# A two-layer transformer on one core: the last tile's rotation and the output weights' split move from the first attention into its projection

## The chip, the core and the metric

The kernel runs on one core of a Trainium2 chip. The metric is the device time of one execution in microseconds (us). The engines are named as in the profile: PE does matrix multiplies, DVE, ACT and POOL do elementwise work, SP starts DMA transfers. They run side by side and wait for each other by semaphores.

## What is computed

Two pre-norm layers, each with attention and a feed-forward block, on x of 2 x 512 tokens x 512, all in float32:

```python
x = L0_attn_x
x = x + _L0_attn_ref(_layernorm(x), Wq, Wk, Wv, Wo)
x = x + _L0_ffn_ref(_layernorm(x), ...)      # gated, low-rank corrections
x = x + _L1_attn_ref(_layernorm(x), ...)     # 32 heads of 128
x = x + _L1_ffn_ref(_layernorm(x), ...)      # gated
```

The change lies in the first of these lines. There, with 32 query heads and 8 key-value heads of 16:

```python
q, k, v = x @ Wq, x @ Wk, x @ Wv             # split into heads
q, k = _apply_rope(q, cos, sin), _apply_rope(k, cos, sin)
scores = einsum('bhqd,bhkd->bhqk', q, k_h) / sqrt(16)     # causal mask
ctx = einsum('bhqk,bhkd->bhqd', softmax(scores), v_h)
return ctx @ Wo
```

## The kernel before, in words

The 1024 tokens are 8 tiles of 128 rows (NT = 8; QT = 4 tiles to a batch element). To keep float32 accuracy, each operand of a multiply is held as a rounded high part and the remainder as a low part: ACT copies the high part (`..._hi`), POOL or DVE subtracts it from the original for the low part (`..._lo`), and PE makes three passes.

`project0` (L912 to L1137) is the first stage. DVE takes the moments of the rows (L97 to L102), ACT takes the root, DVE finishes the inverse (L110 to L114) and writes the normalised row of 512 (`ln.rows`, L140). PE transposes it into `p_turned` (L186), ACT and DVE split it into `h0_hi` and `h0_lo` (L170, L153), and PE multiplies with the query columns (`p_qbank`, 512 wide) and with the key and value columns (`p_kvbank`, 256 wide). Moments are taken for pairs of tiles (PARTS). In program order, DVE takes those of tiles 0 to 3 ahead of the first rotation, those of tiles 4 and 5 behind the first, those of tiles 6 and 7 behind the second. Then, tile by tile, DVE rotates the query columns (`rotate_part`, L892, L896, L897: a cosine product in `rot_a`, a sine product in `rot_b`), then the key columns; POOL adds both products over all 640 columns in one instruction (L1134); ACT writes the high parts of query (L1023) and key (L1025) twice; DVE writes the query's low part (`query_low`, L902) and POOL the key's (`key_low`, L909). `rot_a` and `rot_b` have two buffers. `fill` writes the constant columns, on DVE that of `q2` (512 wide, L1066) among them.

The last tile (LATE = 7) is only copied off PSUM by ACT (L1047, L1048). Its rotation is done within `attend0`, on DVE in unit 1 (`late_rotate`), on POOL (L1853, L909), on ACT (L1722, L1724), and its query low on DVE in unit 2.

`attend0` (L1140 to L1868) begins when every engine has left `project0`: each stage is a block, and between two stands a barrier. It works through 8 units (a batch element and two of its key-value heads), in an order that is written out by hand and identical on each engine. A unit has M_ALL = 20 pieces of 128 keys x 512 scores. For each, PE makes the transposed scores, ACT takes the exponential (L1687) and the high part (L1696), POOL the low part (L1849), and PE weighs the values with both (`a_cbank`, L1323). POOL also writes the maxima back as two columns (`put_maxima`, L1821, L1823), four times a unit. Units 0 to 3 need tiles 0 to 3, units 4 to 7 tiles 4 to 7. From unit 5 on, finished tiles are also projected with Wo.

Wo (1 MB) is loaded into the half of `head` that the last tile's rotation uses. So SP waits for that tile (`late_ready`, L1212) before it starts the load. ACT makes the four high parts in units 2 and 3 (L1716), POOL the four low parts (L1860, placed by WO_LOW). The first L1716 stands on ACT's queue behind the first high part of unit 2 and waits for the load.

## Time and profile before

| | us |
|---|---|
| median of 3 runs | 1443.37 (1442.25 to 1444.95) |
| the profiled execution | 1439.98 |
| its span in the trace | 1437.9 |

| engine | busy, us | share |
|---|---|---|
| PE | 1342.3 | 93% |
| DVE | 1005.7 | 70% |
| ACT | 719.3 | 50% |
| POOL | 696.9 | 48% |

The shares are means over stages with different limits. The projection is the span's first 61.9 us, the first attention lasts to about 353 us (POOL's last low part of it ends at 351.75 us), and the rest is not touched by the change. Times of the trace are counted from the start of the span.

### The profile page before, as it was taken

To read this page: it belongs to the slowest core of one execution; us is meant where nothing else is said; L and a number is where in the kernel's file an instruction comes from. 1 tells how busy PE (TensorE), PEld (TensorE's weight loads), DVE (VectorE), ACT (ScalarE), POOL (GpSimd) and SP (SyncE) were. 2 spreads that over 40 slices of the span, in tenths; PEclk is the share of its full clock that TensorE was granted. 3 is DMA by queue.
4 is the path that set the end of the run, shared out by engine and by line. 5 is a ranking of instruction groups with operands and counts; after the bars stand their busy time and mean duration, and the time that the engine had idled before them with its cause. 6 is when DMAs were issued, how large, how long until landed. Compare 5 with 4: busy or idle time off the path is not lost. (4 is left out here: it accounts for less than half of the span.)

```text
span 1437.9 us, 20245 instructions
## 1 busy us (share of the span) xinstructions
PE 1342.3 (93%) x6728; PEld 1078.9 (75%) x6728; DVE 1005.7 (70%) x2372; ACT 719.3 (50%) x1562; POOL 696.9 (48%) x608
## 2 busy tenths in 40 slices
PE   6788999987897799999999999999999998799999
PEld 5665666665675688888888888888888887588887
DVE  7787777774857678777877788777877788522322
ACT  3377886675544355454554445544545455243332
POOL 4488996775442554244442444335424440155453
PEclk9999999999999899999999999999999999999999
DMA  3000000100200111010110101101101010033332
GB/s 110 1 1 31 1 1 1 31 1 15 77 13 12 62 31 45 15 41 19 30 40 13 37 30 30 37 8 31 44 16 44 9 45 0 20 106 90 102 89 83
DMA packets 65382, 50.73 MB, mean 35 GB/s; under 512 B 6208, under 2 KB 54720, under 8 KB 65024
## 3 DMA queue, kind: packets, MB, share of 16 engines
q1 hardware_dynamic: 65280, 49.44, 11.9%
q8 instruction: 55, 0.90, 0.3%
q14 instruction: 47, 0.39, 0.1%
HBM read 47.33 MB, written 2.10 MB: 34 GB/s over the span
## 5 line engine op out<-in xcount | busy, mean ns | idle before, releaser
L1849 POOL TENSOR_TENSOR a_p_lo<-a_prob,a_p_hi 128x512 fp32r<-128x512 f32 x160 | 203.4, 1291 | 51.4 <-ACT a_p_hi L1696 48.9
L234 DVE CUSTOM_DVE_ANT_0 a_score<-a_score,mask_w 128x384 f32<-128x384 f32 (+3 forms) x384 | 196.1, 558 | 17.9 <-PE a_score L1287 10.0
L692 ACT ACTIVATE a_pt_hi<-a_ring 128x512 fp32r<-128x512 f32 x160 | 93.8, 596 | 173.2 <-PE a_ring L401 173.1
L828 POOL TENSOR_TENSOR a_rot_a<-a_rot_a,a_rot_b 128x512 f32<-128x512 f32 x80 | 103.5, 1294 | 139.6 <-DVE a_rot_b L571 139.6
L683 ACT ACTIVATE a_prob<-a_score,a_nmax 128x128 f32<-128x128 f32 (+3 forms) x256 | 131.9, 528 | 59.7 <-DVE a_nmax L234 59.7
L2468 POOL TENSOR_TENSOR f_w_lo<-raw,f_w_hi 128x512 fp32r<-128x512 f32 (+2 forms) x66 | 90.8, 1401 | 141.9 <-ACT f_w_hi L2411 141.8
L344 PE MATMUL a_xo<-h_hi,a_w_hi 128*128 128x512 f32 x384 | 151.3, 394 | 5.3 <-POOL a_w_lo L838 4.2
L346 PE MATMUL a_xo<-h_hi,a_w_lo 128*128 128x512 f32 x384 | 150.8, 393 | 0.0
L345 PE MATMUL a_xo<-h_lo,a_w_hi 128*128 128x512 f32 x384 | 150.2, 391 | 0.0
L833 POOL TENSOR_TENSOR a_p_lo<-a_rot_a,a_p_hi 128x512 fp32r<-128x512 f32 x80 | 103.3, 1292 | 69.4 <-ACT a_p_hi L709 69.4
L553 DVE TENSOR_TENSOR a_pt_lo<-a_ring,a_pt_hi 128x512 fp32r<-128x512 f32 x160 | 108.4, 686 | 33.5 <-ACT a_pt_hi L692 32.5
L1696 ACT ACTIVATE a_p_hi<-a_prob 128x512 fp32r<-128x512 f32 x160 | 100.1, 630 | 45.9 <-PE a_cbank L1323 44.2
L838 POOL TENSOR_TENSOR a_w_lo<-raw,a_w_hi 128x512 fp32r<-128x512 f32 x48 | 63.0, 1316 | 105.1 <-ACT a_w_hi L720 105.1
L547 DVE TENSOR_SCALAR a_prob<-a_prob,a_rinv 128x128 f32<-128x128 f32 (+3 forms) x256 | 106.6, 459 | 4.8
L344 PE MATMUL a_xo<-a_wo_hi,a_c_hi 128*128 128x512 f32 x256 | 103.0, 402 | 1.4 <-DVE a_c_lo L558 1.4
L709 ACT ACTIVATE a_p_hi<-a_rot_a 128x512 fp32r<-128x512 f32 x80 | 50.4, 630 | 106.8 <-POOL a_rot_a L828 106.8
L843 POOL TENSOR_TENSOR a_wo_lo<-raw,a_wo_hi 128x512 fp32r<-128x512 f32 x32 | 43.0, 1355 | 118.7 <-ACT a_wo_hi L728 118.7
L346 PE MATMUL a_xo<-a_wo_hi,a_c_lo 128*128 128x512 f32 x256 | 100.4, 392 | 0.0
L345 PE MATMUL a_xo<-a_wo_lo,a_c_hi 128*128 128x512 f32 x256 | 100.1, 391 | 0.0
L1687 ACT ACTIVATE a_prob<-a_turned 128x512 f32<-128x512 f32 x160 | 92.7, 589 | 11.5 <-POOL a_p_lo L1849 6.3
L401 PE MATMUL a_ring<-ident,a_prob 128*128 128x128 f32 x640 | 93.6, 272 | 1.1 <-DVE a_prob L547 0.9
L344 PE MATMUL a_score<-a_p_hi 128*128 128x128 f32 (+3 forms) x256 | 88.8, 347 | 5.4 <-POOL a_p_lo L833 4.6
(346 smaller groups left out, 3630.7 us busy)
## 6 DMA issues: line engine op xcount, KB each, us to landing
raw<-in_L_gate_up_t SPq DMA_DIRECT2D x40, 256.0 KB, 3.0
raw<-in_L_attn_wq SPq DMA_DIRECT2D x32, 256.0 KB, 2.8
raw<-in_L_attn_wo SPq DMA_DIRECT2D x32, 256.0 KB, 2.5
raw<-in_L_down_t SPq DMA_DIRECT2D x20, 256.0 KB, 2.7
raw<-in_L_attn_wk SPq DMA_DIRECT2D x8, 256.0 KB, 2.9
raw<-in_L_attn_wv SPq DMA_DIRECT2D x8, 256.0 KB, 2.8
out<-x SPq DMA_DIRECT2D x8, 256.0 KB, 2.4
p_raw_w<-in_L_qkv SPq DMA_DIRECT2D x4, 384.0 KB, 5.7
```

The costliest lines, as they stand in the source:

```text
L234: return nc.vector.tensor_tensor_reduce(scores, scores, m.mask_w[:, T - n:T], -1.0, LARGE, ALU.add, ALU.min, to)
L344: nc.tensor.matmul(out, l_hi, r_hi, start=start, stop=False)
L345: nc.tensor.matmul(out, l_hi, r_lo, start=False, stop=False)
L346: return nc.tensor.matmul(out, l_lo, r_hi, start=False, stop=stop)
L547: last = nc.vector.tensor_scalar(pr, pr, rinv[:, i % 2, h:h + 1], None, ALU.mult)
L553: nc.vector.tensor_tensor(pt_lo[:, n % NPT, :], ring[n % 2][:, :], pt_hi[:, n % NPT, :].bitcast(F32), ALU.subtract).then_inc(ring_read, 1)
L683: nc.scalar.activation(prob[i % 2][:, h, 0:n], score[e % NS][:, (h % per) * n:(h % per + 1) * n], ACT.Exp, bias=nmax[:, i % 2, h:h + 1], s ...
L692: nc.scalar.activation(pt_hi[:, n % NPT, :], ring[n % 2][:, :], ACT.Copy).then_inc(pt_hi_done, 1)
L828: nc.gpsimd.tensor_tensor(rot_a[:, c % 2, :], rot_a[:, c % 2, :], rot_b[:, c % 2, :], ALU.add).then_inc(summed, 1)
L833: nc.gpsimd.tensor_tensor(p_lo[:, u % 2, c, :], rot_a[:, c % 2, :], p_hi[:, u % 2, c, :].bitcast(F32), ALU.subtract).then_inc(p_ready, 1)
L1696: nc.scalar.activation(p_hi[:, mm % NP, :], prob[:, mm % NE, :], ACT.Copy).then_inc(p_hi_done, 1)
L1849: nc.gpsimd.tensor_tensor(p_lo[:, mm % NP, :], prob[:, mm % NE, :], p_hi[:, mm % NP, :].bitcast(F32), ALU.subtract).then_inc(p_ready, 1)
```

## The change

1. Wo leaves `head` for memory of its own: `m.raw_wo`, in whose place `m.wo_lo` is then written, and `m.wo_hi`. This staging area first holds the first two pieces of the query, key and value weights, so SP starts Wo's load as soon as their low parts are made. ACT splits one piece behind each of tiles 1 to 4 of the projection, POOL one behind each of tiles 2 to 5.
2. The last tile is rotated, added and split in `project0` like the others. The late steps in `attend0` and the waits for them are gone.
3. The moments of all 8 tiles are taken ahead of the first rotation.
4. POOL's sum is two instructions, 512 columns of query and 128 of key. The first can start before the keys are rotated, and `query_low` waits for the query's high part alone.
5. To make room, `h0_hi` and `h0_lo` hold 3 tiles instead of 4, so ACT's high part of tile 3 moves behind the first tile's values. The memsets of `q2` move to POOL for tiles 0 to 3, and behind the rotations for tiles 4 to 7.
6. The loads of tiles 4 to 7 are issued ahead of the tables, and the three extra table loads are gone.

Core of the diff:

```diff
-    LATE = NT - 1
...
+        raw_wo = m.raw_wo[:, :, :]
+        early_w, late_w = raw_wo.rearrange("p k n -> p (k n)"), sb("raw_w", [P, 2, W])
+        raw_w = [early_w[:, 0:W], early_w[:, W:2 * W], late_w[:, 0, :], late_w[:, 1, :]]
         w_hi, w_lo = sb("w_hi", [P, KT, W], F32R), sb("w_lo", [P, KT, W], F32R)
-        rot_a = sb("rot_a", [P, 2, QW + KW])
-        rot_b = [m.late_a, m.late_b]
+        rot_a = [sb("rot_a", [P, QW + KW])[:, :], m.late_a]
+        rot_b = m.rot_b
...
             for to, of in ((m.cos0, "c_cos0"), (m.sin0, "c_sin0"), (m.nsin0, "c_nsin0")):
                 sp.dma_start(to[:, :, :], inp[of]).then_inc(tables, 16)
-            for to, of in zip(m.late_tables, ("c_cos0", "c_sin0", "c_nsin0")):
-                sp.dma_start(to[:, :, :], inp[of][:, QT - 1:QT, :]).then_inc(tables, 16)
-            load_x(4, 2)
-            load_x(6, 2)
             sp.dma_start(m.mask[:, :], inp["c_mask"]).then_inc(m.masks, 16)
             sp.dma_start(m.mask_t[:, :], inp["c_mask_t"]).then_inc(m.masks, 16)
+            sp.wait_ge(w_ready, 2)
+            sp.dma_start(raw_wo, wo_v).then_inc(wo_loaded, 16)
...
-                act.wait_ge(summed, t + 1)
-                r = rot_a[:, t % 2, :]
+                r = rot_a[t % 2]
+                act.wait_ge(summed, 2 * t + 1)
                 nc.scalar.activation(m.q2[t][:, :, 0:4:2, :], twice(r[:, 0:QW]), ACT.Copy,
                                      scale=float(HD0) ** -0.5).then_inc(hi_done, 1)
+                act.wait_ge(summed, 2 * t + 2)
                 nc.scalar.activation(m.k2[t][:, :, 0:2, :], twice(r[:, QW:QW + KW]), ACT.Copy).then_inc(hi_done, 1)
...
+            def out_weights_high(k):
+                act.wait_ge(wo_loaded, 16)
+                nc.scalar.activation(m.wo_hi[:, k, :], raw_wo[:, k, :], ACT.Copy).then_inc(wo_hi_done, 1)
...
             weights_high(2)
+            weights_high(3)
             ln.roots(act, 1)
-            weights_high(3)
             ln.high(act, 2)
-            ln.high(act, 3)
+            ln.roots(act, 2)
+            ln.roots(act, 3)
             for t in range(NT):
                 if t >= 1:
...
                 nc.scalar.activation(m.vw[:, t, :, 0, 0:3:2, 0:HD0], v, ACT.Copy)
                 nc.scalar.activation(m.vw[:, t, :, 1, 0:3:2, 0:HD0], v, ACT.Copy).then_inc(v_read, 1)
-                if t < 2:
-                    ln.roots(act, t + 2)
-                elif t + 2 < NT:
+                if t == 0:
+                    ln.high(act, 3)
+                if 2 <= t < NT - 2:
                     ln.high(act, t + 2)
+                if 1 <= t <= KT:
+                    out_weights_high(t - 1)
+            high(NT - 1)
...
             ln.low(dve, 0)
-            fill(2)
             ln.low(dve, 1)
-            for t in range(3, NT):
-                fill(t)
             ln.variances(dve, 1)
             ln.inverses(dve, 1)
             ln.rows(dve, 2)
             ln.rows(dve, 3)
+            fill(6)
+            fill(7)
+            ln.variances(dve, 2)
             ln.low(dve, 2)
-            ln.low(dve, 3)
-            dve.wait_ge(tables, 16 * 6)
+            ln.inverses(dve, 2)
+            ln.variances(dve, 3)
+            ln.inverses(dve, 3)
+            ln.rows(dve, 4)
+            dve.wait_ge(tables, 16 * 3)
             for t in range(NT):
-                if t < LATE:
-                    dve.wait_ge(made, 2 * t + 1)
-                    if t >= 2:
-                        dve.wait_ge(k_ready, t - 1)
-                        dve.wait_ge(q_ready, t - 1)
-                    rotate_part(nc, m, t, qbank[t % 3][:, :], rot_a[:, t % 2, 0:QW], rot_b[t % 2][:, 0:QW]).then_inc(q_rotated, 1)
+                dve.wait_ge(made, 2 * t + 1)
+                if t >= 2:
+                    dve.wait_ge(k_ready, t - 1)
+                    dve.wait_ge(q_ready, t - 1)
+                rotate_part(nc, m, t, qbank[t % 3][:, :], rot_a[t % 2][:, 0:QW], rot_b[t % 2][:, 0:QW]).then_inc(q_rotated, 1)
                 if t >= 2:
                     low(t - 1)
-                if t >= 2 and t + 3 < NT:
-                    ln.rows(dve, t + 3)
+                if t >= 1 and t + 4 < NT:
+                    ln.rows(dve, t + 4)
                 dve.wait_ge(v_read, t + 1)
-                if t < LATE:
-                    rotate_part(nc, m, t, kvbank[t % 2][:, 0:KW], rot_a[:, t % 2, QW:QW + KW],
-                                rot_b[t % 2][:, QW:QW + KW]).then_inc(rotated, 1)
+                rotate_part(nc, m, t, kvbank[t % 2][:, 0:KW], rot_a[t % 2][:, QW:QW + KW],
+                            rot_b[t % 2][:, QW:QW + KW]).then_inc(k_rotated, 1)
                 nc.vector.tensor_tensor(m.vw[:, t, :, 0, 0:3:2, HD0 + 1:2 * HD0 + 1],
                                         kvbank[t % 2][:, KW:2 * KW].rearrange("p (g x n) -> p g x n", x=2, n=HD0),
                                         m.vw[:, t, :, 0, 0:3:2, 0:HD0].bitcast(F32), ALU.subtract).then_inc(v_ready, 1)
-                if t < 2:
-                    ln.variances(dve, t + 2)
-                    ln.inverses(dve, t + 2)
-                    if t == 0:
-                        ln.rows(dve, 4)
+                if t == 0:
+                    ln.low(dve, 3)
                 if t == 1:
                     low(0)
-                elif 2 <= t and t + 2 < NT:
+                if 2 <= t < NT - 2:
                     ln.low(dve, t + 2)
-                if t == LATE - 1:
+                if t >= QT - 1 and t < NT - 1:
+                    fill_queries(t + 1)
+                if t == NT - 2:
                     dve.wait_ge(m.masks, 16 * 2)
                     for to, of in ((m.ident_r, m.ident), (m.ident_b, m.ident), (m.mask_b, m.mask), (m.mask_t_b, m.mask_t)):
...
 
...
+                nc.gpsimd.memset(m.q2[t][:, :, 3, :].bitcast(F32), 0.0)
...
                                         ALU.subtract).then_inc(w_ready, 1)
             for t in range(QT, NT):
                 fill(t)
-            for t in range(LATE):
-                pool.wait_ge(rotated, t + 1)
-                nc.gpsimd.tensor_tensor(rot_a[:, t % 2, :], rot_a[:, t % 2, :], rot_b[t % 2],
-                                        ALU.add).then_inc(summed, 1)
+            for t in range(NT):
+                a, b = rot_a[t % 2], rot_b[t % 2]
+                pool.wait_ge(q_rotated, t + 1)
+                nc.gpsimd.tensor_tensor(a[:, 0:QW], a[:, 0:QW], b[:, 0:QW], ALU.add).then_inc(summed, 1)
+                pool.wait_ge(k_rotated, t + 1)
+                nc.gpsimd.tensor_tensor(a[:, QW:QW + KW], a[:, QW:QW + KW], b[:, QW:QW + KW], ALU.add).then_inc(summed, 1)
                 pool.wait_ge(hi_done, 2 * t + 2)
-                key_low(nc, m, t, rot_a[:, t % 2, :]).then_inc(k_ready, 1)
+                key_low(nc, m, t, a).then_inc(k_ready, 1)
+                if 2 <= t < 2 + KT:
+                    k = t - 2
+                    pool.wait_ge(wo_hi_done, k + 1)
+                    nc.gpsimd.tensor_tensor(m.wo_lo[:, k, :], raw_wo[:, k, :], m.wo_hi[:, k, :].bitcast(F32), ALU.subtract)
 
 
...
-            sp.wait_ge(late_ready, 2)
-            sp.dma_start(raw_wo, wo_v).then_inc(loaded, 16)
...
-                if u == 1:
-                    late_rotate()
...
-                if u == 2:
-                    late_low()
...
-                if 2 <= u < PAIRS:
-                    out_weights_high(2 * u - 4)
...
-                if u == 1:
-                    late_high()
...
-                if 2 <= u < PAIRS:
-                    out_weights_high(2 * u - 3)
...
-                if mm == LATE_SUM:
-                    pool.wait_ge(late_rotated, 1)
-                    nc.gpsimd.tensor_tensor(m.late_a, m.late_a, m.late_b, ALU.add).then_inc(late_summed, 1)
-                if mm == LATE_LOW:
-                    pool.wait_ge(late_hi_done, 2)
-                    key_low(nc, m, NT - 1, m.late_a).then_inc(late_ready, 1)
-                if mm in WO_LOW:
-                    k = WO_LOW.index(mm)
-                    pool.wait_ge(wo_hi_done, k + 1)
-                    nc.gpsimd.tensor_tensor(wo_lo[:, k, :], raw_wo[:, k, :], wo_hi[:, k, :].bitcast(F32),
...
-                m.late_row, m.late_a, m.late_b = (late[:, k * rows:(k + 1) * rows] for k in range(3))
+                m.rot_b = [late[:, k * rows:(k + 1) * rows] for k in range(2)]
+                m.late_a, m.late_b = late[:, 2 * rows:3 * rows], m.rot_b[(NT - 1) % 2]
+                m.wo_hi = ssb("wo_hi", [P, KT, D], F32R)
+                with nc.sbuf_tensor("raw_wo", [P, KT, D], F32) as m.raw_wo:
+                    pass
+                m.wo_lo = ssb("wo_lo", [P, KT, D], F32R)
...
-                    m.h0_hi, m.h0_lo = isb("h0_hi", [P, KT, QT * P], F32R), isb("h0_lo", [P, KT, QT * P], F32R)
+                    m.h0_hi, m.h0_lo = (isb(n, [P, KT, H0_TILES * P], F32R) for n in ("h0_hi", "h0_lo"))
```

DVE in the program before, from the normalised rows of tiles 2 and 3 on:

```order
L140 TENSOR_SCALAR head<-x,n_mv,n_rstd 128x512 x2
L153 TENSOR_TENSOR h_lo<-p_turned,h_hi 128x4x128 x2
L892 TENSOR_TENSOR p_rot_a<-p_qbank,mask_w 128x512
L896 TENSOR_TENSOR head<-p_qbank,mask_w 128x32x8
L897 TENSOR_TENSOR head<-p_qbank,mask_w 128x32x8
L892 TENSOR_TENSOR p_rot_a<-p_kvbank,mask_w 128x128
L896 TENSOR_TENSOR head<-p_kvbank,mask_w 128x8x8
L897 TENSOR_TENSOR head<-p_kvbank,mask_w 128x8x8
L1101 TENSOR_TENSOR vw<-p_kvbank,vw 128x4x2x16
L97 BN_STATS stats<-x 128x6 x2
```

DVE in the changed program, from the end of the scales of tiles 4 and 5 (`n_rstd`, L114) to the first rotation (L892):

```order
L114 TENSOR_TENSOR n_rstd<-n_y 128x2
L97 BN_STATS stats<-x 128x6 x2
L100 BN_AGGR n_mv<-stats 128x2 x2
L102 TENSOR_SCALAR n_ve<-n_mv 128x2
L110 RECIPROCAL n_y<-n_sd 128x2
L111 TENSOR_TENSOR n_y<-n_y 128x2
L112 TENSOR_TENSOR n_y<-n_y,n_ve 128x2
L113 TENSOR_SCALAR n_y<-n_y 128x2
L114 TENSOR_TENSOR n_rstd<-n_y 128x2
L140 TENSOR_SCALAR head<-x,n_mv,n_rstd 128x512
L892 TENSOR_TENSOR p_rot_a<-p_qbank,mask_w 128x512
```

The moments of tiles 4 to 7 and the normalised row of tile 4 (the last L140) stand ahead of the first L892; before, two of these moments (L97 x2) come behind it.

POOL in the program before, tiles 2 to 4 of the projection (L1134 is the sum, L909 the key's low part):

```order
L1134 TENSOR_TENSOR p_rot_a<-p_rot_a,head 128x640
L909 TENSOR_TENSOR f_lo<-p_rot_a,f_lo 128x8x16
L1134 TENSOR_TENSOR p_rot_a<-p_rot_a,head 128x640
L909 TENSOR_TENSOR f_lo<-p_rot_a,f_lo 128x8x16
L1134 TENSOR_TENSOR p_rot_a<-p_rot_a,head 128x640
```

POOL in the changed program, tiles 2 to 4 (L1150 and L1152 are the two sums, L1158 the low part of a piece of Wo):

```order
L1150 TENSOR_TENSOR p_rot_a<-p_rot_a,head 128x512
L1152 TENSOR_TENSOR p_rot_a<-p_rot_a,head 128x128
L909 TENSOR_TENSOR f_lo<-p_rot_a,f_lo 128x8x16
L1158 TENSOR_TENSOR wo_lo<-raw_wo,wo_hi 128x512
L1150 TENSOR_TENSOR head<-head 128x512
L1152 TENSOR_TENSOR head<-head 128x128
L909 TENSOR_TENSOR f_lo<-head,f_lo 128x8x16
L1158 TENSOR_TENSOR wo_lo<-raw_wo,wo_hi 128x512
L1150 TENSOR_TENSOR p_rot_a<-p_rot_a,head 128x512
L1152 TENSOR_TENSOR p_rot_a<-p_rot_a,head 128x128
L909 TENSOR_TENSOR b_st<-p_rot_a,b_st 128x8x16
```

Each tile has one sum more, and behind tiles 2 to 5 stands a piece of Wo, ahead of the next tile's sum.

POOL in the program before, unit 2 of the attention:

```order
L1821 CAST h_lo<-a_nmax 128x8
L1823 TENSOR_TENSOR h_lo<-a_nmax,h_lo 128x8
L1849 TENSOR_TENSOR a_p_lo<-a_prob,a_p_hi 128x512 x4
L1860 TENSOR_TENSOR a_wo_lo<-head,a_wo_hi 128x512
L1849 TENSOR_TENSOR a_p_lo<-a_prob,a_p_hi 128x512 x2
L1821 CAST h_lo<-a_nmax 128x8
```

POOL in the changed program, the same unit:

```order
L1797 CAST h_lo<-a_nmax 128x8
L1799 TENSOR_TENSOR h_lo<-a_nmax,h_lo 128x8
L1825 TENSOR_TENSOR a_p_lo<-a_prob,a_p_hi 128x512 x6
L1797 CAST h_lo<-a_nmax 128x8
L1799 TENSOR_TENSOR h_lo<-a_nmax,h_lo 128x8
```

The piece of Wo between the low parts of this unit is gone (there are four in units 2 and 3).

## Rows read from the trace of the kernel before

**Rows 1.** Stretches of attention: length, busy (count) by engine, PE clock, DMA share

```profile
78.86:108.84 29.98, 26.74 (x152) 18.74 (x151) 24.70 (x63) 23.43 (x44) 27.14 (x29) 1.00 0.00 1
108.84:140.83 31.99, 29.52 (x157) 19.99 (x156) 24.79 (x66) 24.75 (x45) 28.92 (x32) 0.95 0.04 7
140.83:175.54 34.71, 30.35 (x163) 20.73 (x161) 24.44 (x65) 26.47 (x49) 29.13 (x31) 0.95 0.07 26
175.54:205.76 30.22, 27.88 (x160) 19.53 (x159) 23.77 (x65) 24.83 (x46) 29.01 (x32) 1.00 0.00 1
```

**Rows 2.** The same view, two shorter stretches of attention

```profile
199.09:205.76 6.67, 6.21 (x32) 4.16 (x32) 5.43 (x20) 4.80 (x10) 6.59 (x9) 1.00 0.00 0
205.76:227.55 21.79, 20.34 (x123) 14.54 (x122) 16.73 (x41) 18.95 (x35) 19.99 (x23) 1.00 0.00 1
```

**Rows 3.** Waits, 140.83 to 168.64 us: total us, times, longest us

```profile
ACT a_wo_hi L1716 <- DMA head<-in_L_attn_Wo: 4.7, 1, 4.7
POOL a_p_lo L1849 <- ACT a_p_hi L1696: 4.7, 3, 4.3
```

**Rows 4.** Timeline of POOL: start us, us, instruction, [idle before, releaser]

```profile
111.82 1.56 POOL L1853 TENSOR_TENSOR head<-head 128x640 f32<-128x640 f32 x1
...
125.71 0.45 POOL L909 TENSOR_TENSOR b_st<-head,b_st 128x128 fp32r<-128x128 f32 x1
...
150.53 1.29 POOL L1860 TENSOR_TENSOR a_wo_lo<-head,a_wo_hi 128x512 fp32r<-128x512 f32 x1
```

**Rows 5.** Timeline of DVE and SyncE's queue in attention

```profile
99.50 1.57 DVE L896 TENSOR_TENSOR head<-head 128x320 f32<-128x320 f32 x1
...
138.53 0.38 SPq L1213 DMA_DIRECT2D head<-in_L_attn_Wo  x1
```

**Rows 6.** Timeline of PE in the projection and at attention's start

```profile
21.20 0.66 PE L186 MATMUL p_turned<-ident,head 128*128 128x128 f32 x4 [3.21 <-DVE head L140]
...
38.72 0.66 PE L186 MATMUL p_turned<-ident,head 128*128 128x128 f32 x4 [3.31 <-DVE head L140]
...
61.95 0.41 PE L1253 MATMUL a_hbank<-ident,f_hi 128*128 128x128 f32 x2 [2.50 <-PEq L924]
```

**Rows 7.** Timeline of DVE in the projection

```profile
5.50 0.48 DVE L1066 MEMSET h_hi<- 128x512 f32 x1
...
17.51 1.73 DVE L114 TENSOR_TENSOR n_rstd<-n_y 128x2 f32<-128x2 f32 x1
...
19.28 2.31 DVE L140 TENSOR_SCALAR head<-x,n_mv,n_rstd 128x512 f32<-128x512 f32 x2
...
24.96 0.68 DVE L892 TENSOR_TENSOR p_rot_a<-p_qbank,mask_w 128x512 f32<-128x512 f32 x1
...
26.88 1.27 DVE L97 BATCH_NORM_STATS2 stats<-x 128x6 f32<-128x512 f32 x2
...
29.96 0.55 DVE L140 TENSOR_SCALAR head<-x,n_mv,n_rstd 128x512 f32<-128x512 f32 x1
...
36.26 0.69 DVE L892 TENSOR_TENSOR p_rot_a<-p_qbank,mask_w 128x512 f32<-128x512 f32 x1
```

**Rows 8.** Timelines of POOL, ACT and DVE, one tile's cycle

```profile
44.02 1.58 POOL L1134 TENSOR_TENSOR p_rot_a<-p_rot_a,head 128x640 f32<-128x640 f32 x1 [0.82 <-DVE head L897]
...
45.63 1.06 ACT L1023 ACTIVATE h_lo<-p_rot_a 128x1024 fp32r<-128x1024 f32 x1 [2.66 <-POOL p_rot_a L1134]
...
47.02 0.69 DVE L902 SCALAR_TENSOR_TENSOR h_lo<-p_rot_a,h_lo 128x512 fp32r<-128x512 f32 x1 [1.03 <-ACT f_lo L1025]
...
47.07 0.97 POOL L909 TENSOR_TENSOR f_lo<-p_rot_a,f_lo 128x128 fp32r<-128x128 f32 x1 [1.48 <-ACT f_lo L1025]
...
48.86 1.57 POOL L1134 TENSOR_TENSOR p_rot_a<-p_rot_a,head 128x640 f32<-128x640 f32 x1 [0.82 <-DVE head L897]
```

**Rows 9.** A stretch at the attention's start (PE clock: the column before the last two)

```profile
64.00:66.00 2.00, 1.88 (x9) 1.72 (x10) 0.42 (x2) 0.00 (x0) 0.00 (x0) 0.56 0.00 0
```

**Rows 10.** DMA issues: tile, queue, count, KB, us to landing

```profile
head<-in_L_attn_Wo SPq DMA_DIRECT2D x1, 1024.0 KB, 5.2
```

83 lines of the change are left out of this document (29 added, 54 removed).

## The prediction, made before the changed kernel ran

> **What bounds the kernel now.** I read the page first. The table of engines puts PE at 93% of the span, yet the change takes nothing off PE, so a gain has to come from stretches in which PE waits. The slices of the page place the dips of PE in the first tenth of the span and in the first attention, which is where the edits lie. The view by stretches is next, cut at the POOL instruction that opens `put_maxima` of a unit's third query tile (one of four in a unit, so the same point each time). Units 0 to 3 of the attention take 29.98, 31.99, 34.71 and 30.22 us, 126.9 together, for the same set of scores [rows 1]. POOL is busy 27.1 to 29.1 us in each and PE 26.7 to 30.4: the two are close to each other, and in unit 3 POOL has 1.2 us idle and PE 2.3. So in these units POOL's extra work counts. The view of waits shows the rest of unit 2: ACT waits 4.7 us for the load of Wo, and POOL 4.7 us for ACT behind it [rows 3]. SP issues that load only at 138.53 [rows 5].
>
> In the projection, the timeline of PE is the view. PE stands still 3.21 us ahead of the transposes of tile 2 and 3.31 us ahead of those of tile 5, each time until DVE has written a normalised row [rows 6]. Behind tile 2 the timeline of POOL, ACT and DVE shows a cycle of 4.84 us a tile (44.02 to 48.86): sum, high parts, low parts, key rotation, sum [rows 8]. The stage ends, for the attention, at 61.95, where PE starts again after 2.50 us [rows 6].
>
> **The attention's units.** What a unit costs without extras is not in the trace as a whole, but both halves are. From the opening point to the fourth `put_maxima`, unit 4 takes 21.79; from there to the next unit, unit 3 takes 6.67, with no piece of Wo in either [rows 2]. Together 28.46, four times 113.8, which is 13.1 less than 126.9. By what is removed: POOL loses a sum of 1.56, a key low of 0.45 and four pieces of Wo at 1.29, together 7.2 [rows 4]; the wait of 4.7 goes [rows 3]; DVE loses the late rotation, of which one of three instructions took 1.57 [rows 5]; ACT loses two copies and four pieces. 7.2 and 4.7 make 11.9. Units 1 and 2 also ran at a granted clock of 0.95 [rows 1]; with the stall gone I expect 1.00 there. I take 12.3: between 11.9 and 13.1, since unit 0 keeps part of its own excess (it starts with empty buffers, and POOL did no late work in it). Bounds: 13.1 if every unit reaches 28.46; 6.9 if none gets below unit 0's 29.98 (126.9 less 120.0).
>
> What is late next in a unit is POOL itself (6.59 busy of 6.67 [rows 2]), with PE 0.4 us behind it. The waits for `late_ready` and `wo_ready` at units 4 and 5 had long been met, so their removal is worth nothing; if they had not been met, units 4 on would show it, and they are no longer than their tile projections explain. From unit 4 on I leave the time as it is.
>
> **The projection, start.** DVE no longer writes the constant columns of `q2` before the moments: 7 memsets of 0.48 ahead of tile 2's moments are gone, 3.4 us [rows 7]. The new order meets POOL's low parts of the weights there. Before, the scale of tiles 2 and 3 (L114) took 1.73 us for two numbers a partition, and the rows 2.31 for two [rows 7], beside POOL; alone a row takes 0.55. I let the rows of tiles 2 and 3 end at 18.6 instead of 21.6, 3.0 earlier. That fills PE's 3.21 us, but PE then meets the next hold: the values of tile 0 must be read before `p_kvbank` is free.
>
> Now DVE does all moments first. One pair with its scale runs from 26.88 to 29.96, 3.08 us [rows 7]. Two pairs, a low part of 0.69 (the size of L902 [rows 8]), a row of 0.55 and 0.5 for the small fills make 7.9 from 18.6: the first rotation starts at 26.5, against 24.96 [rows 7]. It is 1.5 late. Until the third rotation DVE needed 11.3 us (24.96 to 36.26 [rows 7]); 6.2 of it are the two pairs, now done, and tile 3's low part of 0.69 comes in, so the third rotation can start at 32.3, 4.0 earlier. The four memsets of 0.48 added behind tiles 3 to 6 lie beside POOL's cycle. The four on POOL lie in its wait for the first weights. ACT's high part of tile 3 stands behind the values of tile 0, and PE needs it only behind tile 2.
>
> **The projection, cycle.** With the sum split, POOL's query sum of a tile starts behind the query rotation, but on POOL's queue behind the key low of the tile before. From the query sum on: 1.29 for 512 columns (as a piece of Wo [rows 4]), 1.47 from the sum's end until the key low starts (45.60 to 47.07, ACT's two copies), and the key low, 0.97 beside DVE [rows 8] and 0.45 alone [rows 4]. That is 3.2 to 3.7, taken as 3.5, and with a piece of Wo of 1.29 behind it 4.5 to 5.0, taken as 4.75. DVE's work in a tile was 3.8 us (4.84 less 1.03 idle [rows 8]); with the memset of 0.48 it stays below that, hidden. So POOL sets the cycle. From 27.9, the end of the first query rotation: two tiles at 3.5, four at 4.75, two at 3.5 make 33.0 and end at 60.9. To PE's next start I add 0.4: 61.3, against 61.95, a gain of 0.7. Bounds: 58.5 with the low prices and a start at 27.0, 63.9 with the high ones and 28.5, so minus 3.5 to plus 2.0.
>
> Behind each piece of Wo on POOL's queue waits the next tile's sum, and behind that DVE, ACT and the end of the stage. PE is not held: it works ahead, with three query banks.
>
> **The clock.** In the stretch from 64 to 66 the granted clock was 0.56 [rows 9], about the lower of its two levels (1.2 GHz), after PE had stood still for 2.50 ahead of 61.95 [rows 6]. In the new order PE has finished tile 7 some 8 us before the attention starts, where it waited 2.50 before. More of the attention's start can run at the lower level: 0 to 2.0 (the 64 to 66 stretch again), and I take 0.5, since in 64 to 66 PE was already slow.
>
> The Trainium skill (TensorE: Matmul & The Clock Gate, section "What's actually happening") says that a monitor halves the array's clock when the array has been idle and restores it under load. By that rule the longer pause costs at the attention's start; by the rows alone the start was slow already. The sum would be 1.5 us higher by the rule in full.
>
> **The sum.** Minus 12.3, minus 0.7, plus 0.5: minus 12.5. The profiled execution took 1439.98, of which 2.1 lie around its span of 1437.9, so it would become 1427.5. The median of the runs, 1443.37, stands 3.4 above it: 1430.9.
>
> **Rivals.**
> 1. PE takes POOL's place. PE has 26.7 us of work in unit 0 [rows 1], and its chains through DVE and ACT may keep a unit at 30.0. Then the units give 6.9 and the whole 7.1: 1436.3. Against it, unit 4's 21.79 stands with PE at 20.34 of it [rows 2]. 15%.
> 2. The projection gains in full: low prices, 58.5, no clock cost, units at 28.46: minus 16.6, 1426.8. For it, PE and DVE have the time; against it, the key lows on POOL already take 0.97 [rows 8]. 15%.
> 3. The projection loses: the late first rotation is not made good and the end is at 63.9, the clock costs 2.0. Then minus 8.3: 1435.1. For it speaks that three steps were added to POOL's cycle. 15%.
> 4. Slower: DVE and POOL hold each other up. The late rotation's L896 took 1.57 beside POOL [rows 5], L114 1.73 [rows 7], the key low 0.97 for 0.45. In the projection, POOL's instructions from the first sum on go from 14 to 28. If each of them waits for one of DVE's (0.52 as the key low) and in each tile one row, low part or memset of DVE waits for a POOL instruction (1.29), the path grows by 3.5 x 0.52 + 1.29 = 3.1 a tile, 25 us over eight tiles, and the kernel stands at 1456. It decides from 15.4 us on, 1.9 a tile. Against it, rotations read PSUM and did not stretch (0.68 at 24.96 [rows 7]). 5%.
> 5. The change doesn't remove the wait for Wo, it moves it: ACT meets it behind tile 1, near 29. SP issues it once two low parts of the projection's weights are made, well before L114 at 17.51 [rows 7], beside which POOL works on the fourth, and the load landed 5.2 us after its issue [rows 10]. If it is late all the same, 4.7 stays: 1435.6. 2%.
>
> Rival 4 is a rule of the Trainium skill (SBUF — State Buffer, section "Who interferes with whom"): a DVE instruction with two inputs from SBUF contends with a GpSimd instruction that reads SBUF, and whoever comes second waits for the whole of the other. The trace agrees in L114 and L896.
>
> **How the numbers follow.** The forecast has 48%. Its own bounds with those of rivals 1 to 3 run from 1426.8 to 1436.3; the joint worst (6.9, plus 2.0, plus 2.0) would be 1440.5. I give 1425 to 1438, which leaves out rival 4, part of the joint worst and a run or two us off in the medians. About 0.2% (2.9 us) is what a measurement of this kernel tells from no change. Faster 92%, within 3%, slower 5% (rival 4).
>
> **What would show it.** Right: the view by stretches of units 0 to 3 gives about 28.5 each, no wait of ACT for Wo's load, POOL above 95% busy; first query rotation near 26.5; POOL's query sums 4.75 apart in tiles 2 to 6; PE's first transpose of the attention at 61.3. Wrong: units near 30 with PE full (rival 1); sums 3.5 apart or PE's start before 59 (rival 2); a start behind 63 (rival 3); rows, low parts and sums stretched beyond 1.3 us one after another (rival 4); a wait of ACT ahead of the pieces of Wo (rival 5).

## The result and the profile after

The changed kernel took 1428.91 us (median of 4 runs, 1428.21 to 1433.82) and the kernel before, in the same series, 1442.81 (4 runs, 1441.41 to 1444.95): ratio 0.9906, 95% interval 0.9882 to 0.9930. It is faster, and the predicted 1430.9 lies 2.0 us above it. A second series of the same two kernels gave 1431.78 and 1442.81, ratio 0.9928 (0.9905 to 0.9951). The sections below say where that scatter is from.

Units 0 to 3 of the attention, cut at the same POOL instruction as in [rows 1], in the view by stretches (stretch, its length, busy time and instructions of PE, PEld, DVE, ACT, POOL, then granted clock, DMA share, GB/s):

```profile
81.47:109.88 28.41, 26.73 (x152) 18.74 (x151) 22.31 (x60) 23.50 (x44) 26.52 (x29) 1.00 0.00 1
109.88:138.31 28.43, 27.65 (x160) 19.48 (x159) 23.71 (x65) 23.91 (x45) 26.57 (x29) 1.00 0.01 2
138.31:166.94 28.63, 27.75 (x160) 19.43 (x159) 23.62 (x65) 24.03 (x45) 26.63 (x30) 1.00 0.00 1
166.94:195.42 28.48, 27.74 (x160) 19.54 (x159) 23.77 (x65) 24.15 (x45) 26.62 (x29) 1.00 0.00 1
```

Together they take 113.95 us where they took 126.90, 12.95 less. The four are alike, at full clock, and the wait for Wo's load is in none of them. The engine that is busiest in them is PE (27.65 to 27.75 of 28.43 to 28.63 in units 1 to 3), ahead of POOL (26.57 to 26.63). The projection, by the timelines of PE, DVE and POOL (start, duration, engine, line, operation; in brackets the idle time before and who ended it); these answer to [rows 6], [rows 7] and [rows 8]:

```profile
61.07 0.66 PE L1264 MATMUL a_hbank<-ident,f_hi 128*128 128x128 f32 x2 [6.00 <-PEq L924]
```

```profile
25.35 0.68 DVE L892 TENSOR_TENSOR p_rot_a<-p_qbank,mask_w 128x512 f32<-128x512 f32 x1
...
31.90 0.69 DVE L892 TENSOR_TENSOR p_rot_a<-p_qbank,mask_w 128x512 f32<-128x512 f32 x1
```

```profile
26.77 1.27 POOL L1150 TENSOR_TENSOR p_rot_a<-p_rot_a,head 128x512 f32<-128x512 f32 x1 [9.82 <-DVE head L897]
...
38.49 1.74 POOL L1150 TENSOR_TENSOR head<-head 128x512 f32<-128x512 f32 x1
41.05 0.46 POOL L1152 TENSOR_TENSOR head<-head 128x128 f32<-128x128 f32 x1 [0.82 <-DVE head L897]
42.04 0.46 POOL L909 TENSOR_TENSOR f_lo<-head,f_lo 128x128 fp32r<-128x128 f32 x1 [0.53 <-ACT f_lo L1028]
42.45 1.30 POOL L1158 TENSOR_TENSOR wo_lo<-raw_wo,wo_hi 128x512 fp32r<-128x512 f32 x1
43.71 1.75 POOL L1150 TENSOR_TENSOR p_rot_a<-p_rot_a,head 128x512 f32<-128x512 f32 x1
...
60.07 0.65 POOL L909 TENSOR_TENSOR b_st<-head,b_st 128x128 fp32r<-128x128 f32 x1 [1.06 <-ACT b_st L1028]
```

PE starts the attention at 61.07 where it started at 61.95, and has stood still 6.00 us by then. The first rotation comes at 25.35, the third at 31.90 (before 36.26). A POOL cycle with a piece of Wo is 5.2 us (38.49 to 43.71); the four of them take 5.15, 5.22, 5.35 and 4.64.

From PE's start to the mark of unit 0 the changed kernel is slower: 61.07 to 81.47 is 20.40, where 61.95 to 78.86 was 16.91. Five of the stretches of that time answer to [rows 9]:

```profile
60.00:62.00 2.00, 0.93 (x5) 0.96 (x6) 0.90 (x2) 0.00 (x0) 1.22 (x3) 0.50 0.00 0
64.00:66.00 2.00, 2.00 (x10) 1.80 (x10) 0.69 (x1) 0.00 (x0) 0.00 (x0) 0.50 0.00 0
70.00:72.00 2.00, 2.00 (x11) 1.72 (x11) 2.00 (x4) 0.00 (x0) 0.00 (x0) 0.50 0.00 0
72.00:74.00 2.00, 1.30 (x7) 0.74 (x5) 0.88 (x3) 1.44 (x2) 0.98 (x4) 0.99 0.01 4
76.00:78.00 2.00, 2.00 (x8) 1.51 (x8) 1.69 (x4) 0.60 (x1) 0.00 (x0) 0.50 0.00 0
```

The granted clock stands at 0.50, TensorE's lower level of 1.2 GHz, from 60 to 72 and again near 77. In the kernel before it was low only from 64 to 68.

The profiled executions add up as follows: the start is 0.9 earlier, the attention's first 20 us are 3.5 longer, and the units are 12.95 shorter, together minus 10.3. A later mark agrees: in its second half, once the weighted values of tiles 0 to 3 are transposed, SP issues a load for the next block (L1216 before, L1229 in the changed kernel). It comes at 264.94 in place of 275.25, the same 10.3. Of that lead 10.1 is left at the last stage (SP's load of the down weights at 1166.08 for 1176.16). There the profiled execution of the changed kernel lost 4.2 us that a second execution of the same kernel did not lose, as the two rows show (first the first execution, then the second):

```profile
1240.00:1256.00 16.00, 13.73 (x48) 11.03 (x49) 8.59 (x22) 7.14 (x13) 6.58 (x6) 0.70 0.30 77
```

```profile
1240.00:1256.00 16.00, 13.80 (x68) 11.05 (x67) 9.30 (x21) 8.49 (x15) 8.56 (x7) 1.00 0.43 111
```

The spans were 1432.0 and 1427.3. The last stage has two lengths in the traces of this study: from SP's first load of the gate weights (1165.11 in the changed kernel) to the end of the span, 14 profiled executions take either 262.6 to 262.9 us (`before`, `again`, `late_back`, `one_sum`, `both`, `both_fill`) or 266.6 to 266.9 (the other eight, the changed kernel's first one among them). So times of one kernel differ by what clock is granted in stages that the change does not touch: of ten runs of the changed kernel, the six with a mean clock of 0.983 to 0.985 took 1427.9 to 1430.4 and the four below 0.980 took 1433.1 to 1437.3. Below I therefore read each experiment first by three marks in its trace: PE's first attention instruction ("start"), POOL's first maximum of the third query tile of unit 0 ("mark"), and SP's load for the next block named above ("end"). The expectations call this last mark the attention's end; it lies inside the attention, which lasts some 76 us more, but behind units 0 to 3. The same kernel run twice gave starts of 61.07 and 61.54, marks 20.40 and 20.36 later, and ends of 264.94 and 265.36; differences under 0.5 us say nothing, and each kernel's marks are from one execution.

### The profile page after: what moved, and what is told of

Same layout as the page of the kernel before. It is cut to its first block and busy times, and to the rows that moved or that the text cites. A ratio compares the mean times of both kernels' runs of the same rounds, so it can differ in the third digit from the quotient of the medians.

```text
span 1432.0 us, 20250 instructions
## 1 busy us (share of the span) xinstructions
PE 1346.9 (94%) x6728; PEld 1085.4 (76%) x6728; DVE 1007.6 (70%) x2371; ACT 718.9 (50%) x1560; POOL 698.3 (49%) x620
## 5 line engine op out<-in xcount | busy, mean ns | idle before, releaser
L235 DVE CUSTOM_DVE_ANT_0 a_score<-a_score,mask_w 128x384 f32<-128x384 f32 (+3 forms) x384 | 196.3, 558 | 20.4 <-PE a_score L1298 12.5
L1681 ACT ACTIVATE a_prob<-a_turned 128x512 f32<-128x512 f32 x160 | 92.7, 588 | 10.3 <-POOL a_p_lo L1825 5.0
```

Source lines behind the costliest of these rows:

```text
L235: return nc.vector.tensor_tensor_reduce(scores, scores, m.mask_w[:, T - n:T], -1.0, LARGE, ALU.add, ALU.min, to)
```

## The experiments

All start from the changed kernel, and their edits are shown in part, with remarks in brackets. Times are medians; ratios are to the kernel before in the same series.

**Unedited, once more** (`again`).

> The changed kernel once more, unedited, in the same rounds as the three kernels beside it; its ratio to the kernel before should be 0.9906 within 0.002, 1428.5 to 1430. It is the base for the others. Its profile answers two questions. Theory A (PE pauses 6 us ahead of the attention and starts it at the lower clock level): the granted clock is near 0.50 from 60 to 72 us here too, and POOL's first maximum of the third query tile comes some 20.4 us behind PE's first instruction of the attention (16.9 in the kernel before). Theory B (that was a chance of one execution): the clock is back at 1.00 by 68 and the stretch is 17 us. The stretch of low clock at 1240 to 1256 us of the first profile, worth 4.2 us, was seen in one execution whose time was 5 us above the other three: I expect it gone, and the span near 1427.

Measured 1431.78, ratio 0.9928 (0.9905 to 0.9951). By the trace this is theory A: the low clock at the attention's start came again, from 61 to 77. The dip at 1240 did not. The median is above the expected 1428.5 to 1430.

**PE kept busy behind its last tile** (`warm`).

```
+            for n in range(22):
+                nc.tensor.matmul(ln.bank[0][:, 0:D], m.h0_hi[:, 0, 0:P], w_hi[:, 0, 0:D], start=True, stop=True)
```

> The changed kernel with 22 matmuls of 512 columns added on PE behind the last tile of the projection; their result is never read. They keep PE busy from 55.0 to about 60 us, where it stood still for 6.0. Theory A (the pause of PE costs the attention's start its clock): the granted clock is 1.00 or nearly so from 60 to 80 us, the 20.4 us from PE's first attention instruction to POOL's mark of unit 0 fall to about 17, and the kernel is 3.0 to 3.5 us faster than the changed kernel. Theory B (the start is longer because of what DVE and POOL do there, or because of data that come late): the clock may rise but the 20.4 us stay above 19.5, and the time is the same within 1 us. Theory C (the clock is held down for another reason than the pause, PE's work having lain under it before too): the clock stays at 0.50 in 60 to 72 and nothing changes.

Measured 1428.09, 0.9895 (0.9871 to 0.9920). Start 60.97, mark 19.25 later, end 263.68: 1.3 us earlier than the changed kernel.

```profile
62.00:64.00 2.00, 0.89 (x7) 0.81 (x7) 1.02 (x2) 0.60 (x1) 0.27 (x1) 0.96 0.08 7
64.00:66.00 2.00, 2.00 (x10) 1.58 (x8) 0.69 (x1) 0.00 (x0) 0.00 (x0) 0.50 0.00 0
76.00:78.00 2.00, 2.00 (x9) 1.46 (x7) 1.57 (x7) 0.73 (x2) 0.00 (x0) 0.62 0.02 4
```

Theory A got a third of what it promised. The clock now held to 64, and then fell all the same. So the pause ahead of the attention is not the whole cause. Whether the 1.1 us are its share is not shown: `wo_back` and `wo_start` below start within 0.02 us of each other and have the mark 20.10 and 18.67 behind.

**POOL's pieces of Wo at the attention's start** (`wo_start`).

```
-                if 2 <= t < 2 + KT:       (POOL, projection: wait and wo_lo piece of tile t - 2)
+            for k in range(KT):           (POOL, attend0, ahead of put_maxima(0, 0))
+                nc.gpsimd.tensor_tensor(m.wo_lo[:, k, :], m.raw_wo[:, k, :], m.wo_hi[:, k, :].bitcast(F32), ALU.subtract)
```

> The changed kernel with POOL's four low parts of Wo moved from the projection's cycle (behind the key lows of tiles 2 to 5) to POOL's idle time at the start of the attention, ahead of its first maxima (it stood still from 62.4 to 68.1 and from 68.6 to 72.7). Theory A (POOL's queue sets the projection's cycle, and each piece costs it what it takes): the gaps between query sums fall from 5.2 to about 3.6 to 4.2 (PE or DVE next), the projection ends 4 to 6 us earlier for the attention, and of that the four pieces at 1.3 that now stand ahead of the first maxima cost 0 to 1; the kernel gains 3 to 5 us over the changed kernel, less if PE, which then has less of a lead, starts the attention at another clock. Theory B (the projection's cycle is set by the chain through DVE and ACT, with POOL's piece beside it): the gaps fall by less than 0.5 us and the kernel gains under 1.5 us. Theory C (DVE's work at the attention's start contends with the pieces there): the projection ends earlier, but POOL's mark of unit 0 does not, and the time is the same.

Measured 1428.85, 0.9903 (0.9884 to 0.9922). Start 58.53, mark 18.67 later, end 260.68: 4.3 us earlier than the changed kernel. Of these 2.5 are the projection; the rest came with the clock, which was back at 1.00 by 70 without a second fall. That a move of POOL's pieces brings this rest is not shown. The pieces fit where POOL waited before:

```profile
59.80 4.94 POOL L1801 TENSOR_TENSOR wo_lo<-raw_wo,wo_hi 128x512 fp32r<-128x512 f32 x4
65.57 0.20 POOL L1793 CAST h_hi<-a_nmax 128x8 fp32r<-128x8 f32 x1 [0.84 <-DVE a_nmax L1503]
```

POOL still waits 0.84 for DVE behind them, and its first maximum comes 7.04 behind the start, as in the changed kernel (68.11 behind 61.07). In the projection four pieces of 1.28 to 1.75 cost 2.5, not 5.2 or more. Without a piece the query sums of tiles 2 to 6 stand 4.55, 5.04, 3.60 and 3.82 apart: POOL then waits for DVE (0.61 and 1.09 us ahead of the sums of tiles 3 and 4). So theory A's "each piece costs it what it takes" is wrong by half.

**All of the split back in units 2 and 3, the load early** (`wo_back`).

```
+    WO_LOW = [2 * M_ALL + 4, 2 * M_ALL + 13, 3 * M_ALL + 4, 3 * M_ALL + 13]
...
+                if mm in WO_LOW:          (POOL, attend0, as before; ACT's copies too)
...
```

> The changed kernel with all eight pieces of the split of Wo (ACT's copies and POOL's low parts) put back into units 2 and 3 of the attention, where the kernel before had them; its load stays early, in the projection, so that nobody waits for it. Theory A (the pieces cost the same wherever POOL is the bound): units 2 and 3 take 2.6 us more each (two pieces at 1.29 on POOL), 31.1 for 28.5, the projection's gaps between sums fall from 5.2 to 3.6 to 4.2 and it ends 4 to 6 us earlier; together minus 1 to plus 1.5 against the changed kernel: the move of the split itself was worth next to nothing, and the gain of the change came from the load's wait (4.7) and the last tile. Theory B (the move is what the change is worth): the projection gains under 1.5 us, units 2 and 3 lose 5.2, and the kernel is 4 us slower than the changed one.

Measured 1432.90, 0.9933 (0.9916 to 0.9949). Start 58.51, end 265.40, the same as in the second run of the changed kernel (265.36).

```profile
107.04:135.48 28.44, 27.68 (x160) 19.45 (x159) 23.71 (x65) 24.57 (x46) 26.57 (x29) 1.00 0.01 2
135.48:165.69 30.21, 27.83 (x160) 19.51 (x159) 23.71 (x65) 25.36 (x47) 29.03 (x32) 1.00 0.00 1
165.69:195.91 30.22, 27.79 (x160) 19.48 (x159) 23.73 (x65) 24.79 (x46) 29.00 (x31) 1.00 0.00 1
```

Two pieces are 2.5 us of POOL in a unit and make it 1.6 to 1.8 longer. The four cost 3.3 there (60.43 for 57.11 in units 2 and 3) and 2.5 in the projection, so moving them was worth 1 us at most. This is theory A, though the pieces are cheaper than it said at both places.

**The same, with the load where it was** (`wo_late`).

```
-            sp.wait_ge(w_ready, 2)        (SP, project0)
-            sp.dma_start(raw_wo, wo_v).then_inc(wo_loaded, 16)
...
+            sp.wait_ge(p_ready, 2 * M_ALL - 1)     (SP, attend0; behind it the same load)
...
```

> The version with the split of Wo back in units 2 and 3 of the attention, and now its load too is issued where the kernel before had it: in the attention, at the end of unit 1, some 0.4 us earlier than ACT needs it. Against the version with the split in the units and the early load, only the moment of the load differs. Theory A (the wait of 4.7 us for the load stood on the path): unit 2 takes 4 to 5 us more (36 for 31.9 of the four stretches, by POOL's marks), the end of the attention 265.4 becomes 269.5 to 270, and the kernel is 4 to 5 us slower than that version. Theory B (the wait was taken out of slack that POOL and PE have in a unit with pieces): less than 2 us. The stall may also cost the clock in unit 2, whose granted clock was 0.95 before: up to 1 us more.

Measured 1435.43, 0.9958 (0.9941 to 0.9974). Unit 2 and its wait (waits: who, for whom, total us, times, longest):

```profile
134.07:169.78 35.71, 30.50 (x160) 21.09 (x159) 24.17 (x65) 26.67 (x49) 29.09 (x31) 0.90 0.07 26
```

```profile
ACT wo_hi L1703 <- DMA raw_wo<-in_L_attn_Wo: 4.4, 1, 4.4
```

35.71 against 30.21: a wait of 4.4 cost 5.5, with the clock at 0.90 in that unit. The end is at 269.53, 4.1 later, for a mark that came 1.4 earlier. The medians differ by 2.5, which is less than the traces' 5.5; the two kernels ran in different series, and the clock of later stages is in both. This is theory A, with its 1 us for the clock.

**The last tile finished in the attention** (`late_back`).

```
+                if u == 1:
+                    late_rotate()         (DVE, unit 1; late_low in unit 2, late_high on ACT)
...
+                if mm == LATE_SUM:        (POOL's sum; its key low at LATE_LOW, as before)
...
```

> The changed kernel with the last tile finished in the attention again (its rows copied by ACT at the projection's end, rotated by DVE in unit 1, summed and parted by POOL in unit 1); the split of Wo stays in the projection. Theory A (the work costs about the same at both places, since POOL is the bound in the units and its cycle sets the projection's end): the projection's end for the attention comes one cycle of 3.3 us earlier, less ACT's two copies of some 1.3, near 58.5 to 59.5 for 61.1; unit 1 takes 2.0 (a sum of 1.56 and a key low of 0.45) to 3.0 us more, 30.5 to 31.5 for 28.4; together minus 0.5 to plus 1. Theory B (the last tile in the units costs more than it does in the projection, since there DVE's rotation also delays maxima): units 1 and 2 take 4 us more and the kernel is 1.5 to 3 us slower.

Measured 1431.97, 0.9926 (0.9905 to 0.9948). Start 58.15 (2.9 earlier), end 266.24.

```profile
77.13:107.19 30.06, 26.79 (x152) 18.78 (x151) 24.75 (x63) 23.47 (x44) 27.20 (x29) 1.00 0.00 1
107.19:139.18 31.99, 29.53 (x157) 19.96 (x156) 24.77 (x66) 25.26 (x46) 28.94 (x32) 0.95 0.01 2
139.18:168.27 29.09, 28.34 (x163) 20.01 (x161) 24.27 (x65) 24.41 (x45) 26.66 (x30) 1.00 0.00 1
```

With 28.45 for unit 3 the four are 119.59. Units 0 and 1 have within 0.1 us the lengths of the kernel before [rows 1]. The late tile costs 5.6 us there (119.59 less 113.95) and 2.9 in the projection, so finishing it there is worth 2.7; the end is only 1.3 later, because the mark came 18.98 behind the start, 1.4 sooner than in the changed kernel. The units follow theory B; the end, at 1.3, lies between the two theories.

**The same without DVE's rotation of it** (`late_norot`). It starts from `late_back` and leaves the last tile's queries and keys unrotated.

```
-                rotate_part(nc, m, NT - 1, m.late_row, m.late_a, m.late_b).then_inc(late_rotated, 1)
+                nc.vector.memset(m.late_b[:, 0:8], 0.0).then_inc(late_rotated, 1)
```

> The version with the last tile finished in the attention, with DVE's three instructions of the late rotation (0.81, 1.57 and 0.48 us in a row, ahead of maxima of unit 1) left out, a memset of 8 columns in their place; the last tile's queries and keys are not rotated. POOL's sum and key low and ACT's copies stay. That version's units took 30.06, 31.99, 29.09 and 28.45 us, 5.8 over four times 28.45, where POOL's two late instructions are only 2.0. Theory A (DVE's rotation delays the maxima, and with them the chain of the next tile; the rest is POOL's): unit 0 falls from 30.06 to 28.5, unit 1 from 31.99 to 30.5; 2.5 to 4 us of the 5.8 go. Theory B (POOL's two instructions and the order in which it waits there cost all of it): unit 0 falls by under 0.5 us and the four units keep 5 or more of the 5.8.

```profile
77.57:105.98 28.41, 26.71 (x152) 18.74 (x151) 22.32 (x61) 23.54 (x44) 26.55 (x30) 1.00 0.00 1
105.98:136.36 30.38, 27.85 (x157) 19.00 (x156) 24.60 (x66) 24.94 (x46) 28.90 (x32) 1.00 0.01 2
```

With 29.07 and 28.43 the four are 116.29. So 3.3 of the 5.6 were DVE's rotation (1.65 in unit 0, 1.61 in unit 1), which lasts 2.86 and stands ahead of maxima; 2.3 were the rest, with POOL's 2.0. Part of the 1.61 is clock: with the rotation PE was busy 0.70 us from 115 to 117, and the granted clock was 0.59 and 0.56 from 117 to 121; without it PE was busy 1.03 there, and the clock stayed at 1.00. This is theory A. One execution took 1432.70.

**The moments back in the loop** (`moments_back`).

```
-            ln.variances(dve, 2)          (and inverses of 2, both of 3, row 4, ahead of the loop)
...
+                if t < 2:                 (behind the value step of tile t)
+                    ln.variances(dve, t + 2)
+                    ln.inverses(dve, t + 2)
...
```

> The changed kernel with the moments of tiles 4 to 7 (variances, ACT's roots, inverses with their scale) and the row of tile 4 back on DVE between the value steps of tiles 0 and 1, and the low part of tile 2 and row order of before with them; all else as changed. Theory A (the prediction: these steps are late there, because DVE is the bound up to the third rotation): the first rotation comes about 6 us earlier than 25.35, but the third lies 0.5 to 2 us later than 31.90 or PE stands still again for tile 5, and PE's first instruction of the attention comes 0.5 to 2.5 us later than 61.1. Theory B (POOL's cycle behind it sets the end and takes up the slack): the first rotation is earlier, POOL's chain of query sums starts earlier by as much, and the attention starts 1 to 4 us earlier than in the changed kernel. Theory C: the end is the same within 0.5 us, since PE, which bounds tiles 2 to 7, ends at 55.0 either way. The marks in the trace decide; the times of these kernels scatter by 5 us with the granted clock of later stretches.

Measured 1430.89, 0.9912 (0.9887 to 0.9937).

```profile
37.27 1.11 PE L186 MATMUL p_turned<-ident,head 128*128 128x128 f32 x4 [4.24 <-DVE head L140]
...
63.59 0.66 PE L1264 MATMUL a_hbank<-ident,f_hi 128*128 128x128 f32 x2 [5.10 <-PEq L924]
```

POOL's query sum of tile 0 starts at 23.31 (26.77 in the changed kernel), that of tile 2 at 35.30 (33.34), and the start at 63.59 is 2.5 later. PE stands still for tile 5 again, as in [rows 6]. This is theory A, though the first rotation came only 3.5 earlier (21.87), not 6. The standstill brings low clock with it: behind it the clock is 0.50 to 0.73 from 36 to 44. The kernel before had 0.58 and 0.56 from 40 to 44, the changed one 1.00 in all of that. How much of the 2.5 is the clock is not separated. The later start does not show in the median; here the mark followed 18.81 later, 1.6 less than in the changed kernel, because the clock came back sooner.

**POOL's sum whole again** (`one_sum`).

```
-                nc.gpsimd.tensor_tensor(a[:, 0:QW], a[:, 0:QW], b[:, 0:QW], ALU.add).then_inc(summed, 1)
-                nc.gpsimd.tensor_tensor(a[:, QW:QW + KW], a[:, QW:QW + KW], b[:, QW:QW + KW], ALU.add).then_inc(summed, 1)
+                nc.gpsimd.tensor_tensor(a, a, b, ALU.add).then_inc(summed, 1)
```

> The changed kernel with POOL's two sums of a tile (512 columns behind the query rotation, 128 behind the key rotation) made one again (640 columns, behind both rotations). Theory A (the split shortens POOL's cycle, because the query sum starts before the key rotation and ACT's high part of the queries beside the second sum): each cycle grows by the wait for the key rotation, 0.5 to 1.5 us, and the attention starts 2 to 6 us later than 61.1 (eight tiles, of which those with a piece of Wo, where POOL comes late anyway, pay least). Theory B (POOL comes late in the cycles with a piece of Wo, so both rotations are done when it gets there, and one instruction of 640 columns costs less than two): the attention starts 0 to 2 us earlier. Theory C: within 0.5 us of 61.1.

Measured 1432.46, 0.9929 (0.9904 to 0.9954).

```profile
41.60 1.56 POOL L1149 TENSOR_TENSOR head<-head 128x640 f32<-128x640 f32 x1
44.64 0.66 POOL L909 TENSOR_TENSOR f_lo<-head,f_lo 128x128 fp32r<-128x128 f32 x1 [1.48 <-ACT f_lo L1027]
45.27 1.29 POOL L1155 TENSOR_TENSOR wo_lo<-raw_wo,wo_hi 128x512 fp32r<-128x512 f32 x1
46.52 1.56 POOL L1149 TENSOR_TENSOR p_rot_a<-p_rot_a,head 128x640 f32<-128x640 f32 x1
```

Start 64.88, 3.8 later; mark and end 3.8 and 3.9 later. This is theory A, but at another place than it said: the cycles with a piece are 4.9 to 5.1 us, for 4.6 to 5.4 with two sums, while tiles 0 to 2 (sums at 27.36, 31.31, 36.51, for 26.77, 29.95, 33.34) and the last two lose. There POOL waits for both rotations and ACT's whole pass.

**The start of the attention with full and with filled pauses** (`both`, `both_fill`, `fill_only`). All three have POOL's pieces at the attention's start. `both` adds 17 matmuls behind PE's last tile, `fill_only` ten in the attention's first unit, `both_fill` has the 17 and the ten.

```
+            for n in range(17):           (PE, behind the last tile of the projection)
+                nc.tensor.matmul(ln.bank[0][:, 0:D], m.h0_hi[:, 0, 0:P], w_hi[:, 0, 0:D], start=True, stop=True)
...
+                if x == 0 and bank == 0 and u == 0 and i < 3:     (PE, ahead of a tile's first scores)
+                    for k in range(4 - (i > 0)):
+                        nc.tensor.matmul(cbank[:, :], wo_hi[:, 0, 0:P], wo_hi[:, 0, :], start=True, stop=True)
```

> The changed kernel with POOL's four low parts of Wo at the attention's start and 17 matmuls of 512 columns behind PE's last tile (results never read), so that PE pauses about 1 us in place of 4.2 ahead of the attention. The version with the move alone had its first attention instruction at 58.5, the mark of unit 0 18.7 us later and the attention's end 4.5 us earlier than the changed kernel; the matmuls alone gave 1.5. Theory A (both gains add, since one is the projection's length and the other the clock's): the low clock starts at 62 in place of 58.5, the mark 17 to 18 us behind the first instruction, attention's end 5 to 6 us earlier than the changed kernel. Theory B (the low clock at the attention's start comes from what PE does there, thin work behind the pause, and only its first 3 us hang on the pause): below 1 us more than the move alone.

> The same, and ten more matmuls of 512 columns whose result is overwritten, in the three places of the attention's first unit where PE waits for ACT or DVE (four ahead of the scores of tile 0, three each ahead of those of tiles 1 and 2). Theory A (the low clock of the attention's start follows PE's pauses there): the granted clock stays at 1.00 from 56 to 80 us or falls for under 2 us, the mark comes 15.5 to 17 us behind the first instruction, and the attention's end is 2 to 3 us earlier than without them. Theory B (it has another cause): the clock falls for 6 us as before, and the ten matmuls, at 0.22 to 0.43 us each, cost 0 to 2 us.

> The version with POOL's four low parts of Wo at the attention's start and the ten filling matmuls in the attention's first unit, but without the 17 behind PE's last tile: PE stands still for 4.2 us ahead of the attention again. With neither, the granted clock was 0.50 from about 59 to 69 us and the mark of unit 0 stood 18.7 us behind PE's first attention instruction; with the 17 alone the clock held until 66 and was 0.50 to 76 (19.6 us); with both it stayed at 1.00 (16.6 us). Theory A (the pause ahead of the attention and the gaps inside its first unit each lower the clock by themselves): the clock falls at about 59 and comes back earlier than without the ten, by 66, with no second dip: 17.5 to 18.5 us, and the kernel is 1 to 2 us slower than with both (1425.5 to 1426.5). Theory B (only the gaps inside the unit count): the clock stays at 1.00, 16.6 us, 1424.5. Theory C (the pause decides, and the ten only add work at the low clock): 18.7 to 20 us, 1428 to 1429.

| kernel | median us | ratio (95%) | start | mark behind it | end |
|---|---|---|---|---|---|
| both | 1424.70 | 0.9876 (0.9856 to 0.9897) | 58.54 | 19.61 | 261.67 |
| both_fill | 1424.48 | 0.9871 (0.9850 to 0.9892) | 59.05 | 16.64 | 259.26 |
| fill_only | 1424.86 | 0.9854 (0.9837 to 0.9871) | 58.57 | 17.38 | 259.49 |

```profile
66.00:68.00 2.00, 2.00 (x12) 1.81 (x11) 2.00 (x4) 0.00 (x0) 0.00 (x0) 0.50 0.00 0
74.00:76.00 2.00, 2.00 (x9) 1.43 (x7) 1.56 (x7) 0.72 (x2) 0.00 (x0) 0.50 0.02 4
```

```profile
56.00:66.00 10.00, 8.20 (x47) 6.11 (x46) 4.76 (x8) 2.56 (x4) 7.88 (x11) 1.00 0.02 2
66.00:76.00 10.00, 8.87 (x46) 5.68 (x44) 8.87 (x26) 5.21 (x9) 2.90 (x7) 1.00 0.01 2
```

```profile
58.00:60.00 2.00, 1.43 (x7) 1.46 (x8) 0.79 (x2) 0.00 (x0) 1.29 (x4) 0.50 0.04 4
62.00:64.00 2.00, 2.00 (x12) 1.79 (x10) 0.55 (x1) 0.00 (x0) 2.00 (x3) 0.56 0.00 0
64.00:66.00 2.00, 1.95 (x12) 1.28 (x10) 0.84 (x2) 0.60 (x1) 1.21 (x3) 1.00 0.00 0
```

The three fences are of `both`, `both_fill` and `fill_only`. With the pause alone filled the clock fell at 66 and stayed at 0.50 to 76, and the end is 1.0 later than in `wo_start`: by the traces theory B, the pause brings nothing when the gaps behind it stay. The median of `both` is 4.1 lower than that of `wo_start` all the same. Its runs had clocks of 0.986 to 0.989 for 0.980 to 0.984, and of the profiled executions that of `wo_start` has the long last stage (266.8) and that of `both` the short one (262.6), in code that neither edit touches. So the 4.1 are not credited to the matmuls; why the runs of `both` were spared is left open. With pause and gaps filled the clock is 1.00 throughout (theory A). With the gaps alone it is low from about 57 to 64 and then back for good, theory A for the clock. Its 1 to 2 us against `both_fill` did not come: the mark is 0.7 farther behind the start, but the 17 matmuls delay that start by 0.5, and the ends are 0.2 apart. With the gaps filled, filling the pause too gained next to nothing. By their ends, 5.4 to 6.1 us ahead of the changed kernel, these last two are the fastest kernels of the study, 18 and 19 us below the kernel before in the median. The three medians cannot be told apart.

## Why the prediction was right, point by point

- **Units, minus 12.3: measured minus 12.95.** The length of 28.46 built from two halves of the trace held (28.41 to 28.63). What I said of the bound did not: POOL, which I wanted above 95% busy, is at 93% and PE at 97%, and no run separates what bounds such a unit. Unit 0 reached it too, where I had left it part of its excess; `late_norot` shows that excess to be DVE's late rotation, which stands in the queue ahead of unit 1's maxima and reaches into unit 0. The breakdown beside it (7.2 of POOL and 4.7 of wait) came near the sum for partly wrong reasons. Measured singly: the wait for the load 5.5 for its 4.4, the four pieces 3.3 for POOL's 5.2, the late tile 5.6 for POOL's 2.0. Those are 14.4, more than the 12.95 they make together; the wait's price is too high by some of that, since unit 2 of `wo_late` took 35.71 at a clock of 0.90 where the kernel before, with more work in it, took 34.71 at 0.95. A likely reason for the rest, not tested, is that POOL has some 1.9 us idle in a unit, which take up part of its extra work, while DVE's 2.86 in a row found no such room. I had listed that rotation at no price.
- **Projection, start.** The rows of tiles 2 and 3 end at 18.2 (18.6 predicted), the first rotation starts at 25.35 (26.5), the third at 31.90 (32.3). Taking the moments early is worth 2.5 at the end.
- **Projection, cycle and end, minus 0.7: measured minus 0.9.** A cycle with a piece took 5.1 in the mean for 4.75, since sums and one piece took 1.64 to 1.75 for 1.27 beside DVE and the key sums of tiles 2 and 3 waited 0.82 for the key rotation. Against that the cycle began 1.1 earlier than taken and tiles 0, 1 and 6 took 3.2 to 3.4 for 3.5. So errors of both signs met near the predicted 60.9 (60.72), which is in part luck. The low bound of 58.5 is also misadded: its prices give 58.2. Undone one at a time, the parts come to: moments early minus 2.5, split sum minus 3.8, last tile plus 2.9, Wo plus 2.5. Their sum, minus 0.9, is what the whole did; with 0.5 of scatter in each, part of that agreement is luck. Of the four the prediction had a price for the pieces of Wo alone, 1.25 each in the cycle; they cost 0.6.
- **The clock, plus 0.5 (0 to 2.0): measured plus 3.5.** This is the term that was mis-sized. I took the start as slow already, expected PE to stand still some 8 us (it was 6.00), and charged the 64 to 66 stretch alone. The traces show low clock for 12 us and a second fall where there were 4. That the low clock is what the 3.5 are is shown by `both_fill`: at 1.00 throughout, the mark stands 16.64 behind the start. I tied the term to the pause, and that is not borne out: with the pause cut to 0.97 (`warm`) and 0.32 (`both`) the mark is still 19.25 and 19.61 behind, and what keeps the clock up is work in the gaps of the first unit. The kernel before has those gaps too and a pause of 2.50, and lost only 4 us of clock; why its fall was so short stays open. Kernels that are alike there reach the mark 18.4 to 20.4 behind their start, after pauses of 2.9 to 9.2 us, so a fall has no fixed price.
- **The sum.** Minus 12.5 was predicted; the traces show minus 10.3 up to the last stage, the medians of two series minus 13.9 and minus 11.0. The median's nearness owes something to chance: the kernel before was profiled at 1439.98 with the short last stage, its median is 2.8 to 3.4 higher, and three of the four runs of the changed kernel in the first series had a clock of 0.984 or 0.985, like its profiled execution without the dip (0.984).
- **Rivals.** 1 (PE in POOL's place, units near 30): PE is the busiest, but the units are at 28.5. 2: no, cycles of 5.2. 3 (projection loses): no, though the clock went past its 2.0. 4 (DVE and POOL hold each other up): it exists, at a seventh of its price or less. Query low parts on DVE took 1.29 and 1.35 for 0.68 and rows 1.51 for 0.53. On POOL's path lie four of eight query sums at 1.64 to 1.75 for 1.27 and one piece at 1.75, 2.2 us together, and the two waits of 0.82 for key rotations that stand behind such rows, for the 25 of the rival. The rule of the Trainium skill (SBUF — State Buffer, section "Who interferes with whom") is seen in the low parts, which read two inputs from SBUF, and would have misled as a time. 5: no, ACT reaches the first piece at 29.66 without a wait.

## What to carry to other kernels

A term for the clock belongs to each edit that moves a pause of PE ahead of a stretch in which PE often waits. Read the stretches on both sides of the seam, and charge the whole start-up of the next stage at the low level as the upper bound; here that start-up took from 16.6 us (clock 1.00 throughout) to 20.4. A stage's extra work is priced by what stands behind it in the queues, not by the busy share of the engine that looks full: 2.86 us of DVE in a row cost 3.3, low clock included, and 5.2 us of POOL in four pieces cost 3.3 too. When the times of one kernel scatter by more than the edit is worth, compare marks in the traces at the seams of the stages.

## What the runs showed of the hardware

The granted clock fell to 0.50, the lower of its two levels, behind a stretch in which PE was busy half of the time, even with a pause of only 0.32 us ahead of the stage (`both`: 1.25 busy of 62 to 64, 0.79 of 64 to 66, the fall at 66). It stayed there while PE was busy 1.3 to 2.0 of each 2 us, until 76. Ten matmuls whose result nobody reads, in waits of 0.7 to 1.1 us, kept it up or brought it back early: the end came 2.4 us earlier in `both_fill` than in `both`, 1.2 in `fill_only` than in `wo_start`. The Trainium skill (TensorE: Matmul & The Clock Gate, section "What's actually happening") says that an idle array loses its clock and load restores it. The trace agrees for the pause of the changed kernel (6.00 us, clock 0.50 at 60); the fall at 66 in `both` came behind work at half load, without such a pause, and the prediction had not foreseen it.
